# Edge counts and weight sums of a graph kernel: a fixed fetch of 128 edges for every five destinations instead of a search through sorted columns

## The reference

```
msg = x[src] * edge_weight[:, None]
agg = jax.ops.segment_sum(msg, dst, num_segments=x.shape[0])
```

## Time and profile before

| | |
|---|---|
| median of three runs | 5692.63 us |
| the profiled execution's own time | 5696.73 us |
| its span, first to last instruction | 5695.1 us |
| PE busy in the span | 4594.2 us (81%) |
| DVE busy | 2710.8 us (48%) |
| ACT busy | 2078.4 us (36%) |
| POOL busy | 863.2 us (15%) |
| mean granted clock of TensorE | 0.892 of full speed |

### The profile page before, as it was taken

How to read it: one execution, slowest core, us unless ns; L and a number is a source line. 1 busy time by engine, 2 the same in 40 slices (tenths; PEclk the granted TensorE clock), 3 DMA queues, 4 the chain that set the end, 5 groups by cost and what they waited for, 6 DMA issues and landing times. The chain is left out here.

```text
span 5695.1 us, 88397 instructions
## 1 busy us (share of the span) xinstructions
PE 4594.2 (81%) x24482; PEld 3867.0 (68%) x24483; DVE 2710.8 (48%) x5117; ACT 2078.4 (36%) x3240; POOL 863.2 (15%) x789
## 2 busy tenths in 40 slices
PE   3788868888865499778689989989759959989766
PEld 2677745555544399548578878778649959979755
DVE  5455567777754400221279779779741131020233
ACT  2333314544442210323256556556524321020232
POOL 2777710000004300002100000000012210000000
PEclk8788879999977799889899999999869979999978
DMA  3433312111122433104211111111022133324100
GB/s 95 115 110 111 99 34 77 71 76 71 76 67 89 119 135 139 31 17 132 66 50 57 38 50 57 43 45 59 26 85 68 65 84 146 144 77 157 59 17 24
DMA packets 150164, 438.51 MB, mean 77 GB/s; under 512 B 25592, under 2 KB 89805, under 8 KB 133676
## 3 DMA queue, kind: packets, MB, share of 16 engines
q1 hardware_dynamic: 115212, 341.23, 16.9%
q0 software_dynamic: 34848, 96.08, 6.0%
HBM read 340.98 MB, written 96.25 MB: 77 GB/s over the span
## 5 line engine op out<-in xcount | busy, mean ns | idle before, releaser
L2448 PE MATMUL p_acc<-p_H,p_eT 125*125 125x256 f32 x3750 | 823.5, 378 | 0.0
L2448 PEld LDWEIGHTS p_acc<-p_H,p_eT 125*125 125x125 f32 x3750 | 695.2, 187 | 106.0
L1033 POOL DMA_INDIRECT p_message<-edge_table,p_index x425 | 502.8, 1183 | 132.2 <-issue 119.7
L1934 DVE BATCH_NORM_STATS2 features_stats<-F x60 | 29.2, 486 | 888.8 <-ACT F L1925 887.3
L1246 PE MATMUL p_acc<-p_message,p_spread 125*125 125x260 f32 x1666 | 423.3, 421 | 28.6 <-issue 28.6
L1705 ACT ACTIVATE p_hid<-p_up,p_b1s 128x125 f32<-128x125 f32 x764 | 272.3, 365 | 397.4 <-PE p_up L1681 353.9
L1246 PEld LDWEIGHTS p_acc<-p_message,p_spread 125*125 125x125 f32 x1666 | 346.8, 210 | 97.3 <-issue 30.5
L1681 PEld LDWEIGHTS p_up<-p_xT,p_w1s 128*128 128x128 f32 x3056 | 377.1, 199 | 51.3 <-issue 33.8
L1681 PE MATMUL p_up<-p_xT,p_w1s 128*128 128x125 f32 x3056 | 384.8, 283 | 32.7 <-issue 12.4
L835 PE MATMUL p_acc<-p_cell,p_heavy 125*125 (+1 forms) x1440 | 401.4, 389 | 0.0
L1298 POOL IOTA p_order_i<- 125x200 int32 x3 | 1.1, 381 | 2441.9 <-SPq L81 2441.9
(11 more groups left out here) (462 smaller groups left out, 8054.7 us busy)
## 6 DMA issues: line engine op xcount, KB each, us to landing
sums_first<-edge_sums SPq DMA_DIRECT2D x48, 1250.0 KB
p_second<-edge_sums SPq DMA_DIRECT2D x48, 1250.0 KB, 7.4
p_count<-edge_counts SPq DMA_DIRECT2D x75, 762.9 KB
edge_sums<-p_sums SPq DMA_DIRECT2D x32, 1250.0 KB
edge_counts<-p_total SPq DMA_DIRECT2D x32, 610.4 KB
p_w1s<-in_L_ffn_W SPq DMA_DIRECT2D x16, 1024.0 KB
p_got<-made SPq DMA_DIRECT2D x25, 560.0 KB
p_dst_all<-dst_row SPq DMA_DIRECT2D x25, 531.2 KB, 3.9
```

What stands on the lines that cost most here:

```text
L1033: pool.indirect_dma_start(message[:, m, k, :], None, table, bass.IndirectOffsetOnAxis(ap=index[:, m, k:k + 1], axis=0)).then_inc(landed[m] ...
L2448: last = pe.matmul(acc[:, s, 0:C], eT[:, r % 4, a % 4], H[:, a, 0:C], start=(a == 0), stop=(a == T - 1))
```

## The change

A block is now five destinations, so 5 * 25 = 125 pairs of destination and hi, and there are 640 blocks in 32 groups of 20. For each block the kernel fetches the 128 edges that begin at the block's first one, by a DMA with an address from a table, so that the edges of a block lie on 128 partitions of one column and a single visit does. The edges lie in DRAM in a new input of four words each (`in_edges`: destination, source, weight, nothing), with 384 empty ones at the end. Edges of later blocks that come along match no cell.

- `load_graph` finds the first edge of each block: it counts the columns that end before it, fetches that column (six indirect DMAs of 125 x 2048 bytes on POOL), counts the edges below, and turns the result into one row, `block_starts`. The table `block_chunks` and its chain of small DVE steps are gone.
- `attend_edges`: SP issues the 640 fetches (650 with the padding), 26 in each of the 25 rounds right behind the load of the round's destinations, to a part of the tile XT that is free then. DVE works out at its start how many blocks have more than 128 edges.
- `count_edges`: a batch is four blocks, 160 batches. DVE builds `low`, `cell` and `heavy` for four blocks with one instruction each, fp32, 128 x 500. TensorE does two fp32 matmuls for a block of 125 columns: `cell` by `low`, so that the counts have destination and hi on partitions, and `heavy` by `cell`. No transposes are left. ACT copies the counts straight to 16 bit and the sums as before. Four buffers and four PSUM banks are used in turn, and two buffers for what is stored. SP stores the counts of a group as 20 x 125 runs of 250 bytes, in two DMAs (112 and 13 partitions).
- Blocks with more than 128 edges are added afterwards, one at a time, in a loop that runs once at least: SP loads the old part of both tables, DVE and TensorE make one more visit, SP stores them back, and loads the next 128 edges. With these inputs no block has more than 128 (the largest has 114), so that its one pass adds nothing.

The core of the diff:

```diff
-BLK = 20
-TB = 5
-GD = TB * BLK
+BLK = 5
+EB = 128
+KB = 4
+BG = 20
+GD = BG * BLK
...
 # load_graph
+            for m in range(6):
+                pool.indirect_dma_start(found[:, m].rearrange("p e k -> p (e k)"), None, edges.rearrange("(c e) k -> c (e k)", e=P),
+                                        bass.IndirectOffsetOnAxis(ap=row[:, m:m + 1], axis=0)).then_inc(found_loaded, 16)
...
 # attend_edges, SP
                 sp.dma_start(dst_all[:, m], dst_row[bass.ds(r * GE, GE)].partition_broadcast(128)).then_inc(dst_loaded[m], 16)
+                for a in range(0, LOADS, LOADS // 2):
+                    b = r * LOADS + a
+                    for k, s in enumerate(g.starts_of(nc, mybir.EngineType.SP, b, LOADS // 2)):
+                        sp.dma_start(own_edges[:, bass.ds(b + k, 1), :].rearrange("p a k -> p (a k)"), edges[bass.ds(s, EB), :]).then_inc(own_edges_loaded, 16)
...
 # count_edges, DVE: one batch
+                dve.wait_ge(batch_used, n + 1)
+                dve.tensor_tensor(low[:, at], lanes, each(lo), ALU.is_equal).then_inc(low_ready, 1)
+                dve.tensor_tensor(cell[:, at], lanes, each(key), ALU.is_equal).then_inc(cell_ready, 1)
+                dve.wait_ge(low_ready, n + 1)
+                dve.tensor_tensor(heavy[:, at], low[:, at], own[:, bass.ds(n * KB, KB), 2:3].bitcast(F32).to_broadcast([EB, KB, P]),
+                                  ALU.mult).then_inc(heavy_ready, 1)
...
 # count_edges, PE: one batch
+                for q in range(KB):
+                    pe.matmul(acc[0:P, at, 0, q * P:(q + 1) * P], cell[:, at, q], low[:, at, q], start=True, stop=not loops, skip_group_check=True)
...
+                    last = pe.matmul(acc[0:P, at, 1, q * P:(q + 1) * P], heavy[:, at, q], cell[:, at, q], start=True, stop=True, skip_group_check=True)
+                last.then_inc(batch_used, 1)
...
 # count_edges, ACT: one batch
+                act.activation(total[:, m, s * KB:(s + 1) * KB].rearrange("p b l -> p (b l)"), acc[0:P, k % BANKS, 0, 0:KB * P], ACT.Copy)
+                act.activation(sums[0:P, m, :, s * KB * BLK:(s + 1) * KB * BLK],
+                               acc[0:P, k % BANKS, 1, 0:KB * P].rearrange("p (b d h) -> p h (b d)", b=KB, h=T), ACT.Copy).then_inc(batch_kept, 1)
...
 # count_edges, SP: a group, and the pass over blocks with more than 128 edges
                     sp.dma_start(weights[bass.ds(j * ROWS, ROWS), :], sums[:, m].rearrange("p h d -> p (h d)")).then_inc(sums_stored[m], 16)
+                    split_rows(sp, table[bass.ds(j * BG, BG)].rearrange("b p l -> p b l"), total[:, m], stored[m])
...
+                sp.dma_start(old_counts[:], old_total).then_inc(old_loaded, 16)
+                sp.dma_start(old_sums[:], old).then_inc(old_loaded, 16)
+                sp.wait_ge(rest_added, v + 1)
+                sp.dma_start(old_total, old_counts[:]).then_inc(rest_stored, 16)
+                sp.dma_start(old, old_sums[:]).then_inc(rest_stored, 16)
+                sp.wait_ge(rest_stored, v * 32 + 32)
```

More of the change, by code:

```diff
@@ L48 @@
 assert ROUNDS * R_CH == CH
-LEAD = 3
 PAD = R_CH + 1
@@ L295, in _ @@
             dve.memset(g.dstf[:], -1.0).then_inc(cleared, 1)
+            then(dve.memset(row[:], 0))
             then(dve.memset(g.zeros[:], 0.0))
@@ L307, in _ @@
             then(dve.tensor_copy(start[:], start_i[:]))
+            then(dve.tensor_copy(g.number[:], number_i[:]))
             dve.wait_ge(joined, 1)
[L311 to L322, removed]
+            for m in range(6):
+                then(dve.tensor_scalar(below[:], ends_all[:, 0], start[:, m:m + 1], None, ALU.is_lt))
+                then(dve.tensor_tensor_reduce(out=scratch[:], in0=below[:], in1=rank[:], scale=1.0,
+                                              scalar=0.0, op0=ALU.mult, op1=ALU.max, accum_out=reach[:, m:m + 1]))
+            dve.tensor_copy(row[0:P], reach[:]).then_inc(reached, 1)
             def prefix(n, total):
@@ new lines, in pick_rest @@
+def pick_rest(dve, then, g, over):
+    then(dve.tensor_scalar(over[:], g.number[:], -1.0, float(BLOCKS), ALU.mult, ALU.add))
+    then(dve.scalar_tensor_tensor(out=over[:], in0=g.rest_edges[:], scalar=0.0, in1=over[:], op0=ALU.is_gt, op1=ALU.mult))
+    then(dve.tensor_reduce(g.pick[:, 0:1], over[:], AX_X, ALU.max))
+    then(dve.tensor_scalar(g.pick[:, 0:1], g.pick[:, 0:1], -1.0, float(BLOCKS), ALU.mult, ALU.add))
+    then(dve.tensor_scalar(g.pick[:, 0:1], g.pick[:, 0:1], float(BLOCKS - 1), None, ALU.min))
+    then(dve.tensor_copy(g.pick_i[:, 0:1], g.pick[:, 0:1]))
@@ L776, in _, with over_batches, rest_total @@
+        def over_batches(eng, one, first=0):
+            with eng.Fori(first, BATCHES // PER) as i:
+                for k in range(PER):
+                    one(i * PER + k, k, i)
+        def rest_total(eng):
+            return eng.value_load(g.pick_i[0:1, 1:2], min_val=1, max_val=CH)
         @block.gpsimd
@@ L789, in _ @@
             then(dve.scalar_tensor_tensor(out=lo[:], in0=hi[:], scalar=-float(P), in1=srcf[:], op0=ALU.mult, op1=ALU.add))
-            then(dve.scalar_tensor_tensor(out=key[:], in0=g.dstf[:], scalar=float(T), in1=hi[:], op0=ALU.mult, op1=ALU.add))
-            for n in range(PARTS_OF):
-                value = g.weight if n == 0 else rest
-                then(dve.tensor_copy(part[:, n], value[:]))
-                if n < PARTS_OF - 1:
-                    then(dve.tensor_tensor(rest[:], value[:], part[:, n], ALU.subtract))
@@ new lines, in _ @@
+            ahead = -(-LOOPED // (BLK * KB * PER))
+            for n in range(ahead * PER):
+                one(n, n % PER, n // PER, True)
+            over_batches(pe, one, ahead)
+            rests = rest_total(pe)
+            pe.wait_ge(batch_kept, BATCHES + BANKS)
+            with pe.Fori(0, rests) as v:
+                pe.wait_ge(rest_made, v + 1)
+                pe.wait_ge(rest_step, v * REST + 11)
+                pe.matmul(acc[0:P, 0, 0, 0:P], rest_cell[:], rest_low[:], start=True, stop=True)
+                pe.matmul(acc[0:P, 0, 1, 0:P], rest_heavy[:], rest_cell[:], start=True, stop=True).then_inc(rest_summed, 1)
+                pe.wait_ge(rest_added, v + 1)
```

422 lines of the change are left out of this document (224 added, 198 removed).

## The result

The changed kernel took 5337.87 us (median of 4 runs, 5333.56 to 5340.99) beside 5697.0 for the kernel before: a ratio of 0.937, interval 0.9353 to 0.9386. The forecast was 5203, with a range up to 5290. The direction holds, but 135 us of the forecast gain are missing. The span shows where: up to the end of X's addition it is 2 us over the forecast, behind the counting 6 us, and the counting itself is 122 us over.

What follows compares the result with a forecast made beforehand. DVE was to bound the new counting loop, POOL the edge attention. Span 5695.1 - 500 (counting) + 10 (edge attention) - 2 (table setup) = 5203 us; range 5165 to 5290.

Steps and rivals of the forecast that it cites:

- PE: 8 fp32 matmuls of 125 columns ... 113 ns each ... 0.91 us a batch: Counting loop: PE's work per batch, priced from fp32 transposes at 113 ns each, takes 0.91 us.
- A PE that falls to the low level would cost ... 22 us at most: Counting loop: PE at 1.2 GHz needs 1.93 us a batch against DVE's 1.79, so 22 us at most.
- rival 1: Counting loop: another engine is slower than DVE, namely ACT's second copy; 97 us more, 5300 us; chance 12%.
- A line between them gives 20 ns for 250 bytes: Counting stores: a 250-byte run costs 20 ns, so a group's stores take 6.6 us and fit in 9.
- Rival 2: Counting loop: the short stores are the bound, 12 us a group, 384 us instead of 305; 5282 us; chance 13%.
- The rearranged copy ... I use 1119: Counting loop: ACT's rearranged copy takes 1119 ns, between 598 and twice 1119, hidden by DVE.
- 1.5 us each: Counting loop: DVE's wait at each of the 8 loop turns, 12 us in all, between 0 and 22.
- the setup: Counting start: from the end of X's addition to the first `low`, 12.5 us instead of 16.5.
- DVE's operation: Counting loop: each 128 x 500 fp32-output operation lasts 682 ns, overlapped to 0.595 us; 1.79 us a batch.
- the pass: Counting end: the single serial pass for blocks over 128 edges takes 27 us, from 15 to 50.
- the table setup: `load_graph`: dropping the block table's chain and adding six indirect DMAs changes the time by -2 us, -6 to +8.
- the lag of the edge attention's first rounds: Edge attention: early loads of `p_dst_all` queue behind 26 fetches each, delaying POOL; +10 us, from 3 to 40.

Runs made afterwards that it cites:

- the run with later loops: Changed kernel with the 125 five-column fp32 self-loop matmuls moved from batches 0 to 31 to batches 60 to 91: 5266.6 us, ratio 0.9234 to the kernel before.
- the third run: Changed kernel without the self loops' matmuls and with counts stored in runs of 5000 bytes: 5205.2 us, ratio 0.9133 to the kernel before.

## Why the prediction was wrong, step by step

A group of the edge attention before, from the page:

```profile
L1246 PE MATMUL p_acc<-p_message,p_spread 125*125 125x260 f32 x1666 | 423.3, 421 | 28.6 <-issue 28.6
```

- **"PE: 8 fp32 matmuls of 125 columns ... 113 ns each ... 0.91 us a batch"** failed. The price came from fp32 transposes, which have one record each: L878 has x800 for 800 of them. An fp32 matmul of two data operands has two here, and that could be read before: L1246 is x1666 for 833 matmuls. At the high clock a batch costs PE 1.75 us (8 x 0.22), level with DVE's 1.77 and not half of it. At the low clock it costs some 3.4 (8 x 0.42).
- **"A PE that falls to the low level would cost ... 22 us at most"** failed with it. By 3.4 us a batch the bound would have been 160 x (3.4 - 1.79), some 260 us, and the range would have had to reach there.
- **The self loops were left out of the sum.** Line L921 stands in the diff, and the kernel before did the same work with 35 bf16 matmuls (L844, 6.3 us). As fp32 work it is still small: at the high clock 31 batches x 0.84 us (2.61 in the run with later loops, less 1.77), about 26 us. At the start it came with a granted clock of 0.50 for 160 us, in place of some 55 us of DVE's time. Taking it away gave some 95 to 100 us with the chip's store rate allowed for, 119 beside the changed kernel's first runs. Why it holds the clock stays open. This is the larger of the two failed sizes, and no rival named it: rival 1 had the right form, another engine slower than DVE, but named ACT.
- **"A line between them gives 20 ns for 250 bytes"** failed by the start of the runs. Aligned, they cost 19 ns; where this kernel puts them, about 45. A group took 10.3 us and not 6.6, the DMA engines were full, and the last stores were late. Rival 2 (12 us a group, 5282) had the mechanism, but gave the shortness as its reason, and the starts are the larger part.
- **"The rearranged copy ... I use 1119"** was too high, at 622 ns, and stayed hidden. **"1.5 us each"** for eight turns was too high by all of it.
- **Right:** the setup (12.9 for 12.5), DVE's operation (0.67 with 0.59 between starts), the pass (22 for 27), the table setup (0 for -2), and the lag of the edge attention's first rounds as described. Its size, +9.7 for +10, is partly luck: POOL waited 19 us longer for PE, and shorter fetches gave half of it back. Luck, too, is that the third run, with both causes gone, took 5205 where the forecast was 5203: its stage is 24 us under the forecast, its attention ended some 8 us over it, and what follows took 15 us longer than before.

## What to carry to other kernels

Count the records of an instruction in the trace before you take its price: an fp32 matmul had two where a transpose had one. Look at the granted clock at the start of a loop: small fp32 matmuls that stood first here cost about 100 us; in bf16 the clock rose early, and 60 batches later they cost about 26. Before pricing short stores by length, look where they start: a pitch of 256 bytes brought the same 250 from 45 to 19 ns.

## What was not expected of the hardware

- PE full for 160 us stayed at a granted clock of 0.50, with one record in three of 5 columns and its weight load of 332 ns among them. The same records, placed where the clock was up, ran at 1.00.
- The same program stored at 205 GB/s on one chip and at 191 on another, in different sets of runs, 20 us in all.
- With the DMA engines full, from 990 us on, the issue of the second count store (13 partitions) held SP for 7 to 10 us; it was 4.8 to 5.1 with aligned starts, and 4.8 to 5.0 in the first regime.
- A 16-bit operand in steps of 128 for 125 made one DVE operation 1789 ns instead of 972.
